# A graph-attention layer on one core: sums in two column halves, a transposing turn, q in two float32r parts, one more tile of 32 on TensorE, a last stage centred by matmul

## What is computed

```python
Qh = (x @ Wq.T + bq).reshape(n, H, D)
Kh = (x @ Wk.T + bk).reshape(n, H, D)
Vh = (x @ Wv.T + bv).reshape(n, H, D)
Ee = (edge_attr @ We.T + be).reshape(-1, H, D)
score = (Kh[src] * Qh[dst] * (1.0 / np.sqrt(D)) * Ee).sum(-1)
score = jnp.exp(jnp.clip(score, -5.0, 5.0))
msg = Vh[src] * score[..., None]
wV = jax.ops.segment_sum(msg, dst, num_segments=n)
return layernorm(x + wV)          # over the 64 features
```

## Time and profile before

| | us |
|---|---|
| median of 3 runs | 1716.46 (1716.1 to 1716.64) |
| the profiled execution | 1715.64 |
| its span, first to last instruction | 1713.8 |
| PE busy | 1649.7 (96%), 13047 matmul instructions |
| DVE busy | 1318.6 (77%) |
| POOL busy | 1263.1 (74%), 1315 gathers of some 948 ns |
| ACT busy | 960.6 (56%) |
| mean granted TensorE clock | 0.98 of full speed |

### The profile page before, as it was taken

The page is one execution under the profiler, slowest core; times in us unless marked ns, Lnnn a source line. Parts: engine busy times, 40 slices in busy tenths (PEclk is TensorE's granted clock), DMA queues, the critical chain, the costliest instruction groups (busy, mean ns, idle before and its releaser), DMA issues. The chain is left out here.

```text
span 1713.8 us, 47297 instructions
## 1 busy us (share of the span) xinstructions
PE 1649.7 (96%) x13047; PEld 1479.4 (86%) x13047; DVE 1318.6 (77%) x2198; ACT 960.6 (56%) x2864; POOL 1263.1 (74%) x1348
## 2 busy tenths in 40 slices
PE   7399999999999999999999999999999999999994
PEld 7298888888888888888888988888888888888884
DVE  6377878778778778778778778778778787787786
ACT  5355555555555556556556556556555555555554
POOL 4677777777777777777777777777777777777774
PEclk8699999999999999999999999999999999999997
DMA  7455554555554555555555555455445555545441
GB/s 240 126 149 132 144 134 131 145 133 132 144 133 133 143 132 135 140 135 135 138 135 137 133 138 139 133 137 138 134 131 145 134 131 144 133 132 145 132 124 62
DMA packets 198830, 234.44 MB, mean 137 GB/s; under 512 B 96742, under 2 KB 123180, under 8 KB 198684
## 3 DMA queue, kind: packets, MB, share of 16 engines
q1 hardware_dynamic: 156732, 147.96, 30.0%
q0 software_dynamic: 42080, 86.26, 20.9%
HBM read 226.67 MB, written 7.38 MB: 137 GB/s over the span
## 5 line engine op out<-in xcount | busy, mean ns | idle before, releaser
L260 POOL DMA_INDIRECT kv<-kv_table,idx x1315 | 1246.1, 948 | 416.5 <-issue 388.1
L654 PE MATMUL xg_bank<-x_hi,src_onehot 128*128 128x448 f32 x2079 | 786.4, 378 | 6.1 <-DVE src_onehot L786 6.1
L655 PE MATMUL xg_bank<-x_lo,src_onehot 128*128 128x448 f32 x2079 | 759.9, 365 | 0.0
L725 ACT ACTIVATE distance<-iota_w,dst_neg 128x64 f32<-128x64 f32 x1612 | 428.4, 339 | 0.0
L654 PEld LDWEIGHTS xg_bank<-x_hi,src_onehot 128*128 128x128 f32 x2079 | 391.8, 188 | 34.6 <-DVE src_onehot L786 6.3
L655 PEld LDWEIGHTS xg_bank<-x_lo,src_onehot 128*128 128x128 f32 x2079 | 392.3, 189 | 27.3
L751 ACT COPY xg_t_sb<-turn_bank 64x256 f32<-64x256 f32 x198 | 61.9, 313 | 616.9 <-PE turn_bank L665 612.1
L798 DVE SCALAR_TENSOR_TENSOR x_sel<-iota_v,src_block,xg_bank 128x448 f32<-128x448 f32 x297 | 202.0, 680 | 248.5 <-PE xg_bank L655 240.7
L786 DVE TENSOR_TENSOR src_onehot<-r_row,xg_bank 128x896 fp32r<-128x896 f32 x297 | 320.0, 1078 | 24.8 <-DMA r_row<-r_table 24.8
L643 PE MATMUL sum_ps<-onehot,msg 128*64 128x64 f32 x3224 | 224.4, 223 | 8.6 <-DVE msg L843 8.6
L643 PEld LDWEIGHTS sum_ps<-onehot,msg 128*64 128x64 f32 x3224 | 208.9, 138 | 17.2 <-DVE msg L843 9.4
(11 more groups left out here) (116 smaller groups left out, 957.8 us busy)
## 6 DMA issues: line engine op xcount, KB each, us to landing
attr_sb<-attr SPq DMA_DIRECT2D x201, 256.0 KB
dst_row<-dst_rows SPq DMA_DIRECT2D x402, 128.0 KB
kv<-kv_table,idx POOLq DMA_INDIRECT x1315
r_row<-r_table SPq DMA_DIRECT2D x99, 128.0 KB
q_win<-q_table SPq DMA_DIRECT2D x404, 24.0 KB
r_row<-r_table SPq DMA_DIRECT2D x99, 64.0 KB
idx<-src_tab SPq DMA_DIRECT2D x206, 4.0 KB, 4.1
kv_table<-kv_stage SPq DMA_DIRECT2D x7, 448.0 KB, 3.8
```

Of the source, the lines that this page charges most:

```text
L260: pool.indirect_dma_start(out=kv[:, slot, t, :], out_offset=None, in_=kv_table, in_offset=bass.IndirectOffsetOnAxis(ap=idx[:, slot, t:t + ...
L654: pe.matmul(xg, src_onehot[:, parity, u, :], x_hi[:, u, :], start=(u == 0), stop=False)
L655: mm = pe.matmul(xg, src_onehot[:, parity, u, :], x_lo[:, u, :], start=False, stop=(u == U - 1))
L725: made = act.activation(distance[:, t, :], iota_w[:, :], ACT.Square, bias=dst_neg[:, ds(g, 1), t:t + 1].rearrange("p o t -> p (o t)"))
```

## The change

- 7 tiles of 32 go to PE instead of 6: `PE_OF` is 2, 2, 2, 1. Since 7 is odd, the two `xg` buffers alternate differently in odd and even rounds, and the loops of PE and DVE have a body of eight steps instead of four, with 24 passes instead of 48.
- `turn_x` uses a transposition. `xg_sb` is padded to 128 columns, of which the upper 64 are zero, so the instruction has 128 weight columns and 128 output partitions.
- `sum_messages` puts even tiles on partitions 0 to 63 of `sum_ps`, odd ones on 64 to 127. `acc` has 128 partitions, and its upper half, zeroed by POOL in the first stage, takes the odd sums.
- q has two float32r parts instead of three bf16 ones; the one-hot `onehot_t` is float32r, and `fetch_q` has two matmuls a pair of tiles. A row of `q_table` is 512 bytes instead of 384.
- In the last stage each block of `acc` is multiplied (f32, 128 partitions, 64 moving columns) with `centering`, twice the matrix I - 1/64 one below the other; that transposes, adds the halves and centres at once. The row sums and the centring on DVE go. ACT squares from PSUM, and DVE does all the scaling, from PSUM.

The diff, without the loops' new arguments:

```diff
@@ -43,15 +43,16 @@
 PE_END = ITERS * SLOTS
-PE_BEFORE = (0, 2, 3, 5)
-PE_EACH = 6
+PE_OF = (2, 2, 2, 1)
+PE_BEFORE = (0, 2, 4, 6)
+PE_EACH = sum(PE_OF)
 Q = PE_EACH * ITERS - PE_SKIPPED
-QROWS = Q // 3
+QROWS = -(-Q // 3)
 assert ITERS * SLOTS < G <= PE_END + SLOTS and TILES % 2 == 0 and SLOTS == 4
-assert BLOCK * V >= N and QROWS * 3 == Q and QROWS <= P
+assert BLOCK * V >= N and QROWS <= P and (ITERS - 2) % 2 == 0 and PE_EACH % 2 == 1
@@ -69,12 +70,12 @@
         kv_table = nc.dram_tensor("kv_table", [NPAD, 2 * F], F32, kind="Internal").ap()
-        q_table = nc.dram_tensor("q_table", [NPAD, 3 * F], BF16, kind="Internal").ap()
-        r_table = nc.dram_tensor("r_table", [1, Q * P], F32, kind="Internal").ap()
+        q_table = nc.dram_tensor("q_table", [NPAD, 2 * F], F32, kind="Internal").ap()
+        r_table = nc.dram_tensor("r_table", [1, QROWS * 3 * P], F32, kind="Internal").ap()
         w_sb = sb("w_sb", [P, 3 * F], F32)
-        acc = sb("acc", [F, NPAD], F32)
+        acc = sb("acc", [P, NPAD], F32)
@@ -86,6 +87,7 @@
         ident = sb("ident", [P, P], F32)
+        centering = sb("centering", [P, F], F32)
@@ -94,15 +96,14 @@
         kv = sb("kv", [P, SLOTS, T, 2 * F], F32)
-        q_win = sb("q_win", [P, SLOTS, 2, 3, F], BF16)
+        q_win = sb("q_win", [P, SLOTS, 2, 2, F], F32R)
-        q_stage = sb("q_stage", [P, NT, 3, F], BF16, first)
-        q_rest = sb("q_rest", [P, 2, CH, F], F32, first)
+        q_stage = sb("q_stage", [P, NT, 2, F], F32R, first)
@@ -229,16 +226,17 @@
         pe_kv_made = sem("pe_kv_made")
+        xg_padded = sem("xg_padded")
         pass_sems = range(attr_loaded[0].num, window_moved.num + 1)
-        assert len(pass_sems) == 6 * SLOTS + 26
+        assert len(pass_sems) == 6 * SLOTS + 27
-            return 0 if isinstance(g, int) and not PE_FROM <= g < PE_END else 2 - slot % 2
+            return 0 if isinstance(g, int) and not PE_FROM <= g < PE_END else PE_OF[slot]
@@ -247,12 +245,16 @@
+        def parity_of(odd, j, k):
+            return ((odd + j // SLOTS) * PE_EACH + PE_BEFORE[j % SLOTS] - PE_SKIPPED + k) % 2
                 return sum(pool_tiles(t * SLOTS + slot, slot) for t in range(turn + 1))
-            return turn * (T - 2 + slot % 2) + pool_tiles(slot, slot)
+            return turn * (T - PE_OF[slot]) + pool_tiles(slot, slot)
@@ -323,6 +325,14 @@
                 pool.wait_ge(iota_set, 5)
+                pool.wait_ge(ident_set, 1)
+                for half in range(2):
+                    rows = slice(half * F, (half + 1) * F)
+                    pool.tensor_scalar(centering[rows, :], ident[rows, rows], -1.0 / F, None, ALU.add)\
+                        .then_inc(centering_made, 1)
+                pool.wait_ge(centering_made, 2)
+                pool.memset(acc[F:P, :], 0.0).then_inc(consts_zeroed, 1)
+                pool.wait_ge(consts_zeroed, 6)
@@ -387,20 +397,13 @@
                     act.wait_ge(x_loaded[c], 16)
-                    act.copy(acc[:, :].rearrange("f (p t) -> f t p", t=NT)[:, c * CH:(c + 1) * CH, :],
+                    act.copy(acc[0:F, :].rearrange("f (p t) -> f t p", t=NT)[:, c * CH:(c + 1) * CH, :],
-                def second_part(c):
-                    act.wait_ge(q_rested, c + 1)
-                    act.copy(q_stage[:, c * CH:(c + 1) * CH, 1, :], q_rest[:, c % 2, :, :]).then_inc(q_part1, 1)
                              .rearrange("p (t f) -> p t f", f=F)).then_inc(q_part0, 1)
-                    if c >= 1:
-                        second_part(c - 1)
-                second_part(CHUNKS - 1)
@@ -466,21 +469,11 @@
-                def third_part(c):
-                    dve.wait_ge(q_part1, c + 1)
-                    dve.tensor_tensor(q_stage[:, c * CH:(c + 1) * CH, 2, :], q_rest[:, c % 2, :, :],
-                                      q_stage[:, c * CH:(c + 1) * CH, 1, :], ALU.subtract).then_inc(q_staged, 1)
                     dve.wait_ge(q_part0, c + 1)
-                    if c >= 2:
-                        dve.wait_ge(q_staged, c - 1)
-                    dve.tensor_tensor(q_rest[:, c % 2, :, :],
+                    dve.tensor_tensor(q_stage[:, c * CH:(c + 1) * CH, 1, :],
                                       bank(q_banks[c % 3], CH * F).rearrange("p (t f) -> p t f", f=F),
-                                      q_stage[:, c * CH:(c + 1) * CH, 0, :], ALU.subtract).then_inc(q_rested, 1)
-                    if c >= 1:
-                        third_part(c - 1)
-                third_part(CHUNKS - 1)
+                                      q_stage[:, c * CH:(c + 1) * CH, 0, :], ALU.subtract).then_inc(q_staged, 1)
@@ -521,11 +514,11 @@
         dst_square = sb("dst_square", [P, PAIRS * P], F32, middle)
-        onehot_t = sb("onehot_t", [P, 2, PAIRS * P], BF16, middle)
+        onehot_t = sb("onehot_t", [P, 2, PAIRS * P], F32R, middle)
         x_sel = sb("x_sel", [P, F, V], F32, middle)
-        xg_sb = sb("xg_sb", [P, 2, 2, F], F32, middle)
+        xg_sb = sb("xg_sb", [P, 2, 2, 2 * F], F32, middle)
@@ -545,9 +538,9 @@
                         base = sp.value_load(base_i[0:1, ds(g, 1)], min_val=0, max_val=BASE_MAX)
-                        rows = q_table[ds(base, W), :].rearrange("n (s f) -> n s f", s=3)
-                        sp.dma_start(q_win[0:W, slot, 0, :, :], rows).then_inc(q_loaded[slot], 16)
-                        sp.dma_start(q_win[W:2 * W, slot, 1, :, :], rows).then_inc(q_loaded[slot], 16)
+                        rows = q_table[ds(base, W), :].rearrange("n (s f) -> n s f", s=2)
+                        sp.dma_start(q_win[0:W, slot, 0, :, :].bitcast(F32), rows).then_inc(q_loaded[slot], 16)
+                        sp.dma_start(q_win[W:2 * W, slot, 1, :, :].bitcast(F32), rows).then_inc(q_loaded[slot], 16)
@@ -629,10 +622,10 @@
                         for k in range(n):
-                            for s in range(3):
+                            for s in range(2):
                                                onehot_t[:, slot % 2, k * P:(k + 1) * P], q_win[:, slot, :, s, :],
-                                               start=(s == 0), stop=(s == 2))
+                                               start=(s == 0), stop=(s == 1))
@@ -640,8 +633,9 @@
                         for t in range(n):
-                            mm = pe.matmul(sum_ps[0:F, slot % 2, 0:W], msg[:, slot % 2, t, :],
-                                           onehot[:, slot, t, :], start=(t == 0), stop=(t == n - 1))
+                            half = slice(t % 2 * F, (t % 2 + 1) * F)
+                            mm = pe.matmul(sum_ps[half, slot % 2, 0:W], msg[:, slot % 2, t, :],
+                                           onehot[:, slot, t, :], start=(t < 2), stop=(t >= n - 2))
@@ -662,7 +656,7 @@
                         for n in range(k):
-                            mm = pe.matmul(turn_bank[0:F, n, :], xg_sb[:, j % 2, n, :], ident[:, :], start=True, stop=True)
+                            mm = pe.transpose(turn_bank[:, n, :], xg_sb[:, j % 2, n, :], ident[:, :])
@@ -688,17 +682,19 @@
                         for k in range(ahead)[1:2]:
-                            gather_x(first_q(i, j + 2) + 1, (PE_BEFORE[(j + 2) % SLOTS] - PE_SKIPPED + 1) % 2)
+                            gather_x(first_q(i, j + 2) + 1, parity_of(odd, j + 2, 1))
+                    pe.wait_ge(xg_padded, 1)
                     for g in range(SLOTS):
-                        step(g, 0, g)
-                    with nc.Fori(1, ITERS - 1, engines=[pe.engine], hint_back_edge=True) as i:
-                        for j in range(SLOTS):
-                            step(i * SLOTS + j, i, j)
+                        step(g, 0, g, 0)
+                    with nc.Fori(0, (ITERS - 2) // 2, engines=[pe.engine], hint_back_edge=True) as two:
+                        for h in range(2):
+                            for j in range(SLOTS):
+                                step(two * (2 * SLOTS) + ((h + 1) * SLOTS + j), two * 2 + (h + 1), j, (h + 1) % 2)
                     for g in range((ITERS - 1) * SLOTS, G):
-                        step(g, g // SLOTS, g % SLOTS)
+                        step(g, g // SLOTS, g % SLOTS, g // SLOTS % 2)
@@ -801,7 +797,7 @@
                             dve.wait_ge(x_turned, g - (PE_FROM + 1))
-                        dve.tensor_reduce(xg_sb[:, j % 2, k, :], x_sel[:, :, :], AX_X, ALU.add).then_inc(x_summed, 1)
+                        dve.tensor_reduce(xg_sb[:, j % 2, k, 0:F], x_sel[:, :, :], AX_X, ALU.add).then_inc(x_summed, 1)
@@ -810,10 +806,10 @@
                             dve.wait_ge(acc_added, g)
-                        dve.tensor_tensor(acc[:, nodes], acc[:, nodes], sum_ps[0:F, slot % 2, 0:W],
+                        dve.tensor_tensor(acc[:, nodes], acc[:, nodes], sum_ps[:, slot % 2, 0:W],
-                    def step(g, i, j):
+                    def step(g, i, j, odd):
@@ -905,8 +901,9 @@
-                        mm = pe.transpose(h_of(c)[:, k, :], acc[:, cols_of(c).start + k:NPAD:NT], ident[0:F, 0:F])
```

(69 more changed lines are left out.)

36 lines of the change are left out of this document (15 added, 21 removed).

## The result

The changed kernel takes 1789.14 us (median of 4 runs, 1787.73 to 1789.91) against 1716.55 (1716.1 to 1718.19) for the kernel before, measured beside it: a ratio of 1.042 [1.0402, 1.0438], slower by 73 us. The forecast was 1800 with a range of 1705 to 1890. The profiled execution took 1789.86 us, its span 1788.0, that is 74.2 more than the span before.

A forecast was written before the change was run, and what follows sets the result against it. PE and POOL were level; after the change PE alone bounds. A round's +3.38 - 1.07 + 0.90 - 1.64 = +1.57 us, times 49, is +77; with -1.2 before the loop and +8.2 after, 1800 us, range 1705 to 1890.

The forecast's parts named there:

- (a): PE's loop round: one more source tile, with a second gather of x, its turn and projection, costs +3.38 us.
- (b): Turn in PE's round: one transposition replaces two f32 instructions, 1.90 us a round, -1.07; bounds -1.3 and 0.
- (c): q in PE's round: eight float32r matmuls at 0.112 us replace twelve bf16 at 0.056, +0.90 us a round.
- (d): Message sums in PE's round: two column halves overlap, nine slots instead of 16, -1.64 us a round.
- The last stage: After the loop: 98 f32 instructions replace 49 transpositions at half clock, 20.9 us with 2.1 behind; +8.2 us.
- The first stage: Before the loop: q's third part goes, with its casts and waits, so x_lo comes 1.2 us earlier; -1.2 us.
- The zeroing of `acc`: First stage: zeroing the upper half falls in POOL's idle time before be_row arrives; hidden, otherwise some us.
- Halves that don't overlap: Rival on the loop's sums: the two halves give no gain, 80 us more, 1880 us; chance 0.22.
- A q at the bf16 pace: Rival in the loop: q's float32r matmuls take 0.056 us each, 88 us less, 1712 us; chance 0.09.
- POOL as the only bound: Rival in the loop: PE's pace hides slack, POOL's queue alone bounds, 61 us less, near 1660; chance 0.03.
- Narrow float32r at the full f32 cost, or a drain at each change of half: Rival in the loop: q's matmuls cost 0.224 us each, 1975 us, or half changes drain PE, 2040; chance 0.14.
- The code fetch at the back edge of the longer body: Rival at the loop's back edge: the eight-step body makes an engine fetch code again; priced at nothing, no chance of its own.

The follow-up runs named there:

- the seventh tile's own run: Changed kernel with f32 turn, q in three bf16 parts and all sums in one half, keeping seven tiles and the new last stage: 1884.87 us, ratio 1.0981.
- the bf16 run: Changed kernel with q again in three bf16 parts, twelve matmuls a step instead of eight: 1760.59 us, ratio 1.0253.
- the last run: Thirteen tiles of 64 on PE, q in bf16, plus matmuls with unread results ahead of the last stage: 1699.2 us against 1715.7 for the kernel before.

## Why the prediction was right

The working forecast +1.57 us a round, and +1.29 came. PE's round did set the time, and the four terms have the sign and about the size that the forecast gave them. The total came out 10 us high, because the loop was put 13 us too high and the first stage 3 and the last 1 us too low. By its steps:

**(a) The seventh tile**, +3.38. With today's turn, q and sums it was 3.22 in the seventh tile's own run. The difference is the size of what the gather matmuls do, which stand 0.202 apart now (824.32 - 821.90 = 2.42 us for 12 gaps) and 0.2035 before (808.19 - 805.75 = 2.44 by the same rows); over the 98 of a round that is some 0.16. In the seventh tile's own run they stand as close, so none of the three other edits is the reason. Why they are closer isn't known.

**(b) The turn**, -1.07 forecast, -0.80 by its own run, -0.85 by the rows: from the last gather matmul to the first sum it is 824.84 - 824.32 = 0.52 with two tiles and 0.56 with one, 3 x 0.52 + 0.56 = 2.12 a round where I had 1.90, against 2.97 in the old way; of the 0.56 some 0.1 is the wait for `msg`. This term was mis-sized, and its step is "0.122 each, at half clock, so about 0.062 at full clock if it scales". Two transpositions start 0.38 - 0.27 = 0.11 apart. I had halved the time for the clock and forgotten that those of the last stage move 64 columns and the turn's move 128. That twice the columns take back what twice the clock gives fits both rows, but no run shows it: the weights differ too, 64 rows in the last stage and 128 in the turn. A nearer row was there, the old turn itself, at full clock and with 128 moving columns: its four f32 instructions take 818.32 - 817.83 = 0.49 us, 0.12 each. So a transposition costs what one f32 instruction does, and the gain is that it is one where there were two. That the stretch with two tiles came out near all the same (0.52 for 0.49) is luck: the 0.08 that I took off for overlap was a guess, and more than that overlapped.

**(c) q**, +0.90 forecast, 4 x 0.17 = +0.68 by the rows (from the first edge matmul to the gather's second 821.90 - 819.91 = 1.99 us, against 805.75 - 803.93 = 1.82 before). The pace was right: (1.09 - 0.28) / 7 = 0.116 between starts. What I left out is the hand-over from the f32 edge matmuls to q, shorter to a float32r matmul (0.81 us from first to first for eight) than to a bf16 one (0.89 in the bf16 run). The bf16 run gives 28.5 us for the whole edit, 0.56 a round, since part of its gain is lost in waits for `msg`. By the runs this is the term that was furthest off.

**(d) The sums**, -1.64 forecast, 4 x (0.62 - 1.02) = -1.60 by the rows, and 84.9 us by difference of the runs, for which I had 80. By their single records the instructions now start in pairs (at 840.370 and 840.377, then at 840.477 and 840.484); in the kernel before they stand 0.058 apart throughout. The trace doesn't name the half; that a pair is one of each half is read from this. The Trainium skill, TensorEngine Tiling (Array Packing), Key Properties, says that different tiles can load weights and multiply in parallel; the trace agrees, with 0.62 in place of 1.02, and adds that the order should alternate (0.89 otherwise). The eight changes of half cost nothing that shows, also as that page has it.

By the rows this is 3.38 - 0.85 + 0.68 - 1.60 - 0.16 = 1.45 in the round shown, measured 1.35 there. By the runs' rounds, against the mean of 33.58, it is 3.22 - 0.79 + 0.56 for the tile, the turn and q, so -1.70 is left for the sums.

**The last stage**, +8.2 forecast, +9.2 in the trace and in its own run. The mechanism (98 instructions for 49, at half clock) was right; the 98 took 1783.50 - 1761.74 = 21.8 us for 20.9, and 2.2 us followed for 2.1. The Trainium skill, TensorE: Matmul & The Clock Gate, Part 1, says that sustained activity releases the clock; the trace disagrees for this kind of matmul: 0.50 through 21.8 us of f32 matmuls with 64 moving columns.

**The first stage** was wrong in sign: -1.2 forecast, +1.8 came (PE's first edge matmuls stand at 66.50 instead of 64.67). The forecast counted the casts that go and nothing else. The chain runs through DVE and POOL. The first load of the middle stage (SP) follows POOL's seventeenth gather, the last of the first stage. In the kernel before, DVE's last wide instruction, the gather under way beside it, the last gather and the load:

```profile
49.81 1.89 DVE L504 SCALAR_TENSOR_TENSOR dst_neg<-base_f,minus_general,dst_neg 128x1616 f32<-128x1616 f32 x1
50.00 2.52 POOL L260 DMA_INDIRECT kv<-kv_table,idx  x1 [0.30 <-issue]
...
56.56 0.94 POOL L260 DMA_INDIRECT kv<-kv_table,idx  x1 [0.30 <-issue]
60.94 0.34 SPq L540 DMA_DIRECT2D attr_sb<-attr  x1
```

In the kernel after:

```profile
51.89 1.90 DVE L497 SCALAR_TENSOR_TENSOR dst_neg<-base_f,minus_general,dst_neg 128x1616 f32<-128x1616 f32 x1
52.08 2.52 POOL L262 DMA_INDIRECT kv<-kv_table,idx  x1 [0.30 <-issue]
...
58.64 0.94 POOL L262 DMA_INDIRECT kv<-kv_table,idx  x1 [0.30 <-issue]
63.01 0.34 SPq L533 DMA_DIRECT2D attr_sb<-attr  x1
```

With six tiles:

```profile
50.17 1.90 DVE L497 SCALAR_TENSOR_TENSOR dst_neg<-base_f,minus_general,dst_neg 128x1616 f32<-128x1616 f32 x1
...
60.69 0.95 POOL L262 DMA_INDIRECT kv<-kv_table,idx  x1 [0.30 <-issue]
65.05 0.34 SPq L533 DMA_DIRECT2D attr_sb<-attr  x1
```

The gather beside DVE's instruction is stretched (2.52 us for the usual 0.94, 2.08 with six tiles) and ends 0.8 us behind it, in these three kernels and in every other run; then the remaining gathers follow at 1.248 us, and 4.3 to 4.4 us behind the start of the last one comes the load. Before and after, four gathers remain, so the 2.1 us (63.01 - 60.94) are DVE's delay, 51.89 - 49.81. It goes back to x_hi, which ACT starts at 44.70 where it started at 42.62, and to the second part of q ahead of it, which PE begins at 32.02 instead of 28.68. Ahead of that DVE writes the tables of source rows, which grow with the seventh tile, from 23.92 to 31.35 (7.43 us) where it took 22.06 to 28.01 (5.95). With six tiles x_hi is back at 42.61. The growth of these tables is work of step (a) that I did not count.

The zeroing of `acc`, called hidden, holds POOL from 17.39 to 22.72, and the first gather starts 1.3 us later. In the kernel after this costs nothing: four gathers remain as before. With six tiles the first gather starts at 30.13 instead of 25.38, seven remain, and the load comes 4.1 us later than in the kernel before. How much of that start is the zeroing no run tests alone.

**The rivals.** Halves that don't overlap would have given 0 for (d); the runs give 84.9 us. A q at the bf16 pace: the 0.116 excludes it. POOL as the only bound: it now waits 123.6 us for `msg`. Narrow float32r at the full f32 cost, or a drain at each change of half: excluded by the rows for (c) and (d). The code fetch at the back edge of the longer body shows in no hole of PE's timeline; one such edge lies in every two rounds, and their difference of 0.12 us is the wait for `msg`.

The 74.2 us of span: 1.8 at the start of the middle stage, 64.1 from there to the edge matmuls of the last two groups, which the trace has at 1747.52 where they stood at 1681.63, 9.2 in the last stage, and 0.9 less in the steps and stores between and behind these.

## What to carry to other kernels

When two engines are level, a whole unit of work moved from one to the other can be too much: count what one unit costs each, and look for the fraction that leaves both below today's pace (here thirteen tiles of 64 instead of seven of 32). Count narrow f32 and float32r matmuls by what loading their weights costs (0.112 us with 64 moving columns, 0.116 with 128, both with 128 weight columns), not by their number; and where weights have 64 columns, put independent sums in two column halves and alternate between them. Before a row is scaled to another clock, look for one of the same form at that clock. And follow a stage back from its end before saying what an edit in it gives: here DVE's growing tables were on the chain, and a count of q's casts alone missed them.

## What the runs showed of the hardware

- f32 instructions with 64 weight and 64 moving columns start in pairs where the column halves alternate: sixteen take 0.62 us so, 0.89 with one half after the other, 1.02 in a single half.
- Transpositions of f32 start 0.11 us apart with 128 moving columns at full clock, and 0.122 with 64 at half clock; f32 matmul instructions with 128 moving columns 0.12 apart at full clock.
- The granted clock stays at 0.50 through PE's whole part of the last stage, 21.8 us of f32 matmuls with 64 moving columns that leave no hole, also where it was 1.00 half a microsecond before that stage (1668 to 1669 of the last run) and fell while PE waited.
- A gather of 128 rows by GpSimd takes 0.94 us alone, and 2.1 to 4.0 us beside a wide DVE instruction (x_lo or dst_neg) in the first stage; it ends 0.8 us behind that instruction.
- Eight float32r matmuls of 128 columns (0.116 apart) take longer than twelve bf16 ones (0.056 apart).
